# Feed forward of a decoder layer: rows transposed by DMA instead of TensorE, seven banks for gate and up, roundings on ScalarE

## The reference

```python
def _weight_quant(w):
    scale = 1.0 / clip(mean(abs(w)), 1e-05)
    return clip(round(w * scale), -1.0, 1.0) / scale
def _act_quant(x):
    scale = 127.0 / clip(max(abs(x), axis=-1, keepdims=True), 1e-05)
    return clip(round(x * scale), -128.0, 127.0) / scale
def _bitlinear(x, w):
    return einsum('bsi,oi->bso', _act_quant(x), _weight_quant(w))
gate = silu(_bitlinear(x, w_gate))
up = _bitlinear(x, w_up)
return _bitlinear(gate * up, w_down)
...
x = _layernorm(x + _L0_ffn_ref(x, L0_ffn_w_gate, L0_ffn_w_up, L0_ffn_w_down), axis=-1)
```

## Time and profile before

| | |
|---|---|
| runs | 1810.21, 1814.68 and 1814.8 us, median 1814.68 |
| the profiled execution | span 1810.6 us; the page gives no time of it beside the span |
| TensorE | busy 1764.0 us, 97% of the span |
| VectorE, ScalarE, GpSimd | 1422.3, 1182.3, 1120.8 us |
| critical chain by engine | PE 71%, issue 10%, POOL 7%, DVE 6%, DMA 4%, ACT 2% |
| TensorE's granted clock, mean | 0.995 of full speed |

### The profile page before, as it was taken

How to read it: one execution, slowest core, us unless ns; L and a number is a source line. 1 busy time by engine, 2 the same in 40 slices (tenths; PEclk the granted TensorE clock), 3 DMA queues, 4 the chain that set the end, 5 groups by cost and what they waited for, 6 DMA issues and landing times.

```text
span 1810.6 us, 43108 instructions
## 1 busy us (share of the span) xinstructions
PE 1764.0 (97%) x14196; PEld 1488.3 (82%) x14213; DVE 1422.3 (79%) x3304; ACT 1182.3 (65%) x2709; POOL 1120.8 (62%) x1250
## 2 busy tenths in 40 slices
PE   8999999999998899999999999999999999989997
PEld 7777777777777899999999999889999999975553
DVE  6777778787887677777777788777777777788998
ACT  6878887756755566666666667666666665665665
POOL 3434445664566586686686655678778778552554
PEclk9999999999998999999999999999999999999999
DMA  5222223111105422432432523314313341552221
GB/s 205 76 65 91 96 81 114 43 30 43 48 21 172 136 93 95 150 98 76 150 103 70 168 92 86 112 50 123 94 60 99 95 115 48 124 110 50 70 70 64
DMA packets 107012, 166.89 MB, mean 92 GB/s; under 512 B 29900, under 2 KB 65104, under 8 KB 106944
## 3 DMA queue, kind: packets, MB, share of 16 engines
q1 hardware_dynamic: 88408, 129.75, 23.3%
q0 software_dynamic: 14656, 28.92, 5.8%
q10 hardware_dynamic: 3880, 7.35, 1.3%
HBM read 109.25 MB, written 50.46 MB: 88 GB/s over the span
## 4 chain that ended last, share of the span: by engine, by line
PE 71%; issue 10%; POOL 7%; DVE 6%; DMA 4%; ACT 2%; POOLq 0%; ACTq 0%; DVEq 0%
PE att_ps_P L1737 5%; PE att_ps_SA L1761 5%; PE att_ps_T L554 5%; PE att_ps_P L1725 4%; PE att_ps_P L1789 4%; PE att_ps_P L554 3%; PE att_ps_O L1725 3%; PE att_ps_T L1725 3%; DMA ca_ct<-ct_kept 3%; PE att_ps_T L1737 3%; PE att_ps_SB L616 3%; POOL sa_p_lo L425 3%; PE att_ps_P L1775 3%; PE att_ps_SB L602 2%; PE att_ps_O L1737 2%
## 5 line engine op out<-in xcount | busy, mean ns | idle before, releaser
L1543 POOL TENSOR_TENSOR ca_pr<-ca_pr,ca_rec 112x750 f32<-112x750 f32 x256 | 366.5, 1452 | 186.4 <-DVE ca_rec L2023 183.3
L425 POOL TENSOR_TENSOR sa_p_lo<-sa_pr,sa_p_hi 112x448 fp32r<-112x448 f32 x128 | 147.1, 1164 | 210.0 <-ACT sa_p_hi L722 209.2
L1908 ACT ACTIVATE ca_big<-att_ps_P 126x384 fp32r<-126x384 f32 (+1 forms) x254 | 105.3, 449 | 66.2 <-PE att_ps_P L1775 64.8
L1902 ACT ACTIVATE ca_pr<-att_ps_SA,ca_nmax 112x750 f32<-112x750 f32 x128 | 113.7, 888 | 21.8 <-DVE ca_nmax L2019 11.0
L891 DVE RECIPROCAL sa_sums<-sa_sums 128x224 f32<-128x224 f32 x64 | 99.1, 1548 | 34.8 <-ACT sa_sums L731 34.6
L2028 DVE TENSOR_TENSOR ca_big<-att_ps_P,ca_big 126x384 fp32r<-126x384 f32 (+1 forms) x254 | 120.0, 500 | 6.2 <-ACT ca_big L1908 5.9
L2019 DVE TENSOR_REDUCE ca_nmax<-att_ps_SA 112x1 f32<-112x752 f32 x128 | 119.2, 931 | 1.3 <-PE att_ps_SA L1761 1.2
L2019 DVE TENSOR_REDUCE ca_nmax<-att_ps_SB 112x1 f32<-112x752 f32 x128 | 119.2, 931 | 0.0
L1737 PE MATMUL att_ps_P<-ca_w_hi,ca_ct 128*126 128x256 f32 x558 | 114.1, 283 | 1.4 <-DVE ca_q_lo L2002 1.4
L1902 ACT ACTIVATE ca_pr<-att_ps_SB,ca_nmax 112x750 f32<-112x750 f32 x128 | 113.3, 885 | 0.1
L1775 PEld LDWEIGHTS att_ps_P<-att_ident,ca_pr 64*126 64x126 f32 (+1 forms) x1524 | 85.8, 138 | 14.6 <-issue 10.8
(11 more groups left out here) (355 smaller groups left out, 6688.7 us busy)
## 6 DMA issues: line engine op xcount, KB each, us to landing
ct_kept<-ca_ct SPq DMA_DIRECT2D x8, 1134.0 KB, 8.9
ca_ct<-ct_kept POOLq DMA_DIRECT2D x8, 1134.0 KB, 8.0
ct_kept<-ca_ct SPq DMA_DIRECT2D x8, 1116.0 KB, 11.5
ca_ct<-ct_kept POOLq DMA_DIRECT2D x8, 1116.0 KB, 10.4
sa_xin<-in_x_dram SPq DMA_DIRECT2D x16, 448.0 KB, 3.6
xt_kept<-ca_xt SPq DMA_DIRECT2D x8, 896.0 KB, 5.2
ca_xt<-xt_kept POOLq DMA_DIRECT2D x8, 896.0 KB, 5.0
ternary<-ca_stage SPq DMA_DIRECT2D x36, 172.0 KB, 1.9
```

Source lines behind the costliest of these rows:

```text
L425: pool.tensor_tensor(p_lo[:, h % NB, :], pr[:, h % NB, :], f32(p_hi[:, h % NB, :]), ALU.subtract).then_inc(p_split, 1)
L1543: pool.tensor_tensor(w, w, rec[:, h % PB, c:c + 1].to_broadcast([R, S]), ALU.mult).then_inc(norm_done, 1)
L1902: act.activation(pr[:, h % PB, c, :].rearrange("r (a s) -> r a s", a=2), two_halves(psum[slot]), ACT.Exp, bias=nmax[:, h % PB, c:c + 1], a ...
```

## The change

In the feed forward only:

- Rows are transposed by transposing DMAs in SyncE's queue: turn_x (xq into one of two buffers xqt) for tiles 2 to 13, turn_hidden (each half of hq into hqt) for tiles 0 to 12. Tiles 0 and 1 still get x by TensorE, tile 13 its hidden rows (transpose_last, copy_last).
- Gate products have four banks, up products three: up 1 and up 3 share P1. A bank is used again by the same product of the next tile.
- The second half of hq is rounded by ScalarE (quantise_second), and from tile 3 on both steps of the rounding of x.
- The scales of all tiles have places of their own (amax, xscale, x_unit, hmax, hscale, h_unit by tile). res, y and y_out move to other addresses.
- The loops of VectorE, ScalarE, TensorE and SyncE are written out tile by tile. GpSimd's loop and its code stay. The new order on VectorE starts each pass with the residual and bn_stats of tile t - 2, and ends it with the aggregate and the guess.
- Some semaphores that only counted turns are merged or left out.

```diff
+    gate_ps = [psum["SB"][:, BANK:2 * BANK], psum["P0"], psum["SA"][:, BANK:2 * BANK], psum["O"]]
+    up_ps = [psum["T"], psum["P1"], psum["SB"][:, 0:BANK], psum["P1"]]
...
+    def before_x(t):
+
+        return xqt_in[(t - 1) % 2], 16 * ((t - 1) // 2)
...
+        def load_x(t):
+            if t:
+                sp.wait_ge(xr_done, t)
+            sp.dma_start(xin[:, :], x2[t * P:t * P + P, :]).then_inc(x_in, 16)
+
+        def load_residual(t):
+            sp.wait_ge(y_summed, t + 1)
+            sp.dma_start(res[:, :], x2[t * P:t * P + P, :]).then_inc(res_in, 16)
+
+        def turn_x(t):
+            sp.wait_ge(xq_done, t + 1)
+            sp.wait_ge(up_filled, FB * (t - 1))
+            sp.dma_start_transpose(xqt[:, t % 2], xq[:, :]).then_inc(xqt_in[t % 2], 16)
+
+        def turn_hidden(t, half):
+            sp.wait_ge(hq_done[half], t + 1)
+            if half == 0:
+                sp.wait_ge(y_filled, t + 1)
+            sp.dma_start_transpose(hqt[:, half * FC // 2:(half + 1) * FC // 2, :], hq[:, half_of(half)]).then_inc(hqt_in[half], 16)
...
         def load_fourth():
...
+            load_x(3)
+            turn_x(2)
+            turn_hidden(0, 0)
+            turn_hidden(0, 1)
 
         def rest():
...
+            for t in range(1, T):
+                if t > 1:
+                    turn_hidden(t - 1, 0)
+                load_residual(t - 1)
+                if t > 1:
+                    turn_hidden(t - 1, 1)
+                if 4 <= t + 3 < T:
+                    load_x(t + 3)
+                if t + 2 < T:
+                    turn_x(t + 2)
+            load_residual(T - 1)
...
         def gate_up(t, first, blocks):
...
+                    if not first and n == 7:
+                        pe.wait_ge(h_done, FB * t + 2)
+                    elif not first and n == 3:
+                        pe.wait_ge(h_done, FB * t)
+                    elif not first:
+                        pe.wait_ge(used, FB * (t - 1) + f + 1)
...
+        def rest():
+            pe.wait_ge(sg_done, FB)
+            for f in range(FB):
+                for ca_done in ca_free(f"v{f}"):
                     pe.wait_ge(*ca_done)
+                gate_up(1, False, [f])
+            pe.wait_ge(held[2], 16)
+            down(0)
+            for t in range(2, T):
+                gate_up(t, False, range(FB))
+                down(t - 1)
+            transpose_last()
             down(T - 1)
...
+        def quantise_second(t):
+            act.wait_ge(h_scaled, 2 * t + 2)
+            if t:
+                act.wait_ge(hqt_in[1], 16 * t)
+            act.activation(hq[:, half_of(1)], h[:, half_of(1)], ACT.Copy, bias=-ROUND).then_inc(hq_done[1], 1)
...
         def rest():
             copy_x(1)
...
+            for t in range(1, T):
+                scale_hidden(t - 1, 0)
+                scale_hidden(t - 1, 1)
+                quantise_second(t - 1)
+                silu(t, 0)
+                silu(t, 1)
+                if t + 2 < T:
+                    round_x(t + 2)
+                silu(t, 2)
+                if t + 2 < T:
+                    quantise_x(t + 2)
+                silu(t, 3)
...
+        def scale_of_hidden(t):
+            links.need(largest(t, 1))
+            links.link(dve.scalar_tensor_tensor(hmax[:, t, 0:1], hmax[:, t, 0:1], 1e-5, hmax[:, t, 1:2], ALU.max, ALU.max))
+            inverse = links.mark(dve.reciprocal(hscale[:, t:t + 1], hmax[:, t, 0:1]))
+            dve.tensor_scalar(h_unit[:, t:t + 1], wmean[:, 2:3], hmax[:, t, 0:1], 1.0 / 127.0, ALU.mult, ALU.mult)
+            links.need(inverse)
+            dve.tensor_scalar(hscale[:, t:t + 1], hscale[:, t:t + 1], 127.0, None, ALU.mult).then_inc(hscale_done, 1)
...
+        def sum_rows(t):
+            dve.wait_ge(y_free, t + 1)
+            add_residual(t, y)
+            dve.wait_ge(y_summed, t + 2)
+            dve.wait_ge(y_done, t + 1)
+            return links.mark(dve.bn_stats(stats[:, 0, :], y[:, :]))
+
+        def guess_root(sums):
+            dve.memset(rs[:, :], 0.0)
+            links.need(sums)
+            links.link(dve.bn_aggr(mv[:, 0, :], stats[:, 0, :]))
+            links.link(dve.tensor_scalar(mv[:, :, 1], mv[:, :, 1], LN_EPS, None, ALU.add))
+            links.link(dve.tensor_scalar(newton[:, :].bitcast(I32), mv[:, :, 1].bitcast(I32), 1, None, ALU.logical_shift_right))
             dve.tensor_scalar(rs[:, :].bitcast(I32), newton[:, :].bitcast(I32), -1.0, RSQRT_GUESS, ALU.mult, ALU.add).then_inc(guess_done, 1)
...
         def rest():
...
+            for t in range(2, T):
+                sums = sum_rows(t - 2)
+                if t + 2 < T:
+                    scale_of_x(t + 2)
+                hidden(t, 0)
+                hidden(t, 1)
+                hidden(t, 2)
+                largest(t, 0)
+                hidden(t, 3)
+                scale_of_hidden(t)
+                guess_root(sums)
+                quantise_hidden(t, 0)
+            quantise_hidden(T - 1, 1)
```

More of the change, by code:

```diff
@@ L2447, in copy_h, with silu @@
-        def copy_h(t, blocks):
-            for q in blocks:
-                act.wait_ge(ht_filled, FB * t + q + 1)
+            act.activation(xqt[:, t], xt_ps[:, :].rearrange("p (k n) -> p k n", k=KC), ACT.Copy).then_inc(xqt_done, 1)
+        def silu(t, f, first=False):
+            if f == 0:
+                act.wait_ge(x_scaled, t + 1)
+            act.wait_ge(gate_filled, FB * t + f + 1)
+            if FB * t + f >= 2:
+                act.wait_ge(h_done, FB * t + f - 1)
+            act.activation(sg[:, f % 2, :], gate_up_bank(f, 0, first)[:, :], ACT.Silu, scale=x_unit[:, t, 0:1]).then_inc(sg_done, 1)
@@ L2452, in copy_h @@
                 act.activation(hqt[:, 4 * q:4 * q + 4, :], ht_ps[q % 2][:, :].rearrange("p (k n) -> p k n", k=4),
                                ACT.Copy).then_inc(hqt_done, 1)
-        def scale_h(t, ahead=False):
-            act.wait_ge(hscale_done, t + 1)
-            for half in range(2):
-                if half and ahead:
-                    silu(t + 1, False, [0])
-                part_h = h[:, half * F // 2:(half + 1) * F // 2]
-                act.activation(part_h, part_h, ACT.Copy, scale=hscale[:, 0:1], bias=ROUND).then_inc(h_scaled, 1)
@@ L2534, in quantise_h, with quantise_hidden, add_residual @@
+        def quantise_hidden(t, half):
             dve.wait_ge(h_scaled, 2 * t + half + 1)
[L2535 to L2537 removed]
+            if t:
+                dve.wait_ge(hqt_in[half], 16 * t)
+            dve.tensor_scalar(hq[:, half_of(half)], h[:, half_of(half)], -ROUND, None, ALU.add).then_inc(hq_done[half], 1)
+        def add_residual(t, rows):
             dve.wait_ge(res_in, 16 * t + 16)
@@ L2592, in first @@
         def first(name):
             if name == "x":
-                dve.memset(h_unit[:, :], 0.0).then_inc(h_unit_clear, 1)
-                chain.step(lambda per, k: k)
                 scale_of_x(0)
             elif name == "xq":
+                round_x(0)
                 quantise_x(0)
-                take_unit(0)
             elif name == "next":
@@ L2602, in first @@
             elif name == "nextq":
-                dve.wait_ge(xt_filled, 1)
+                round_x(1)
                 quantise_x(1)
             elif name == "h":
-                dve.wait_ge(h_unit_clear, 1)
-                finish_h(0, statistics=False, next_hidden=False)
-            elif name == "v2":
-                chain.step(lambda per, k: FIRST + k)
-                hidden(1, 2)
-                largest(1, 0)
+                scale_of_hidden(0)
+                scale_of_x(2)
+                quantise_hidden(0, 0)
+                round_x(2)
+                quantise_x(2)
             elif name == "g":
-                finish_h(1, statistics=False)
+                scale_of_hidden(1)
+                quantise_hidden(1, 0)
             elif name[0] == "v":
-                dve.wait_ge(unit_done, 2)
-                hidden(1, int(name[1]))
+                f = int(name[1])
+                if f == 1:
+                    scale_of_x(3)
+                hidden(1, f)
+                if f == 2:
+                    largest(1, 0)
             else:
@@ L2621, in first @@
                     largest(0, 0)
[L2623 to L2649 removed]
+        def rest():
+            for t in range(2, T):
[11 more added lines that the diff above has]
+            quantise_hidden(T - 1, 1)
+            for i, rows in enumerate(last_rows):
+                t = T - 2 + i
+                add_residual(t, rows)
                 dve.wait_ge(y_summed, t + 2)
[L2651 removed]
+                layernorm(dve, links, [rows[:, :]], stats, last_mv, last_rs[:, :], last_newton[:, :], last_done)
         return first, rest
```

315 lines of the change are left out of this document (105 added, 210 removed).

## The result

The changed kernel took 1855.72 us in the median of four runs (1854.55 to 1856.46), the kernel before 1814.74 in the runs beside it; the ratio is 1.0234 with an interval of 1.0217 to 1.0251. The change costs 41 us. The profiled execution took 1856.46 us, its span is 1854.9.

A forecast was written before the change was run, and what follows sets the result against it. Bound now: TensorE; after: a ring of VectorE and GpSimd waits, 8.4 + 0.1 + 6.4 + 0.15 = 15.05 us a tile. Span 1810.6 + 43.4 = 1854.0, plus 4.1 to the median: 1858 us, range 1849 to 1876.

The forecast's parts named there:

- ring: Feed-forward loop: VectorE's guess, GpSimd's chain, next bn_stats, whole pass; 15.05 us a tile against 11.48; forecast given 0.82.
- The cover: Feed-forward loop: TensorE idle about 4.8 us a tile; half 1's transpose has 7.8 us against 4 taken.
- The start: Hand-over into feed forward: VectorE stands about 0.9 us for x; residual here at 1664.6, tile 0's bn_stats at 1665.4.
- The end: After the feed-forward loop: last scale done at 1838.65 against 1795.27; tail the same program, 15.3 us; span 1854.0.
- low bound of the range: Whole kernel: 1849, with -3 for the ring and 4 us either way for the loop's start and end.
- VectorE's busy time: Feed-forward tile: 10.56 less 0.68 for one hq rounding and some 1.2 for other work, 8.7 us.
- rival (a): Feed forward: the y_done wait costs nothing, TensorE stays the bound; 11 us less, 1804; chance 0.06.
- Transposes: SyncE's transposing DMAs: 0.14 us of queue a block; 4 us for half the hidden rows, bounds 1.5 and 9.
- Rival (b): Feed forward: transposing DMAs become the bound; worst 27 us a tile, about 2000; by the skill's price some 1990; chance 0.05.
- The clock: Feed-forward TensorE, idle 4.8 us a tile: some microseconds at half clock, +0.2 us a tile, in the upper end.
- rule weighed in the prediction: Feed-forward TensorE: idle gaps between matmul bursts send its clock to half rate, each tile begins slow; sum 1860.
- upper end: Feed-forward loop: includes +0.2 us a tile for TensorE's down products finishing later at half clock; sum 1860.

The follow-up runs named there:

- wait-moved version: Changed kernel with VectorE's wait for y_done moved from ahead of bn_stats to ahead of guess_root: 1810.4 us against 1813.9 for the kernel before, ratio 0.9973.

## Why the prediction was right

The forecast was 1858 us and a ring; 1855.7 came, by that ring.

- **Ring.** Forecast 15.05 us a tile, 15.10 in the mean. VectorE's part 8.4, measured 8.55: the third silu and h 3 came 0.1 later. GpSimd 6.4, measured 6.50, and 0.20 for two semaphores where 0.25 was put in. Two experiments on the length of GpSimd's chain, one on the wait and two on the kernel before show that it is this ring and the order that closes it.
- **The cover.** VectorE is ready at 1736.81 + 0.74 and waits to 1741.91; TensorE waits for h 1 ahead of the last up product. Forecast 4.8 us of idle TensorE, measured 3.4 in the mean of twelve waits (1.7 to 4.9), as its matmuls behind the lull were slower:

```profile
...
1729.94 1.89 PE L2420 MATMUL att_ps_P<-ff_held,ff_xqt 128*128 128x512 bf16 x4 [2.94 <-DVE ff_h L2574]
...
1731.62 4.10 PE L2443 MATMUL att_ps_SA<-ff_held,ff_hqt 128*128 128x512 bf16 x16
...
```

- **The start.** The residual's load: forecast 1661.07 + 0.9 = 1661.97, issued at 1662.51; bn_stats of tile 0 forecast at 1665.4, came at 1666.0. These 0.6 us, and ten passes of 15.2 against 15.05 (+1.7), are made up for by passes 12 and 13, which have no x to prepare and are 1.1 us shorter each; this I had not taken out. That the last scale was forecast to 0.02 us is luck: these errors cancel.
- **The end.** The last scale was to be done at 1838.65, it was at 1838.52 + 0.15 = 1838.67. From there to the end of the span it took 16.2 us, not 15.3: TensorE had stood 2.43 us ahead of the last transposes (1.06 in the kernel before), its clock fell to 0.50, and the 16 matmuls of down(13) took 4.70 us where they had taken 3.62.

```profile
...
1841.07 0.40 PE L2431 MATMUL att_ps_SB<-ff_ident_b,ff_hq 128*128 128x128 bf16 x4 [2.43 <-DVE ff_hq L2593]
...
1843.05 4.70 PE L2443 MATMUL att_ps_SA<-ff_held,ff_hqt 128*128 128x512 bf16 x16
```

```profile
...
1842.00:1844.00 2.00, 1.75 (x11) 1.14 (x12) 1.77 (x8) 1.68 (x4) 1.44 (x8) 0.50 0.29 80
...
```

The span came out at 1854.9 against 1854.0, 0.9 us longer than forecast. To get from the span to the median I added 4.1 us, and the median lay 0.8 above the profiled span: 3.3 too much. The two errors partly cancel and leave the 2.3 us by which 1858 was over. The low bound of the range was not what its terms give: 1858 - 3 - 4 is 1851, not 1849.
- **VectorE's busy time** was put at 8.7 us a tile and was 9.8. 0.45 us of the difference is its rounding, 1.13 us where 0.68 was put in; where the rest comes from I have not worked out. The forecast didn't hang on it, since the ring was added up from its own steps, but rival (a) did: with the ring opened VectorE's queue came to 10.83 us a tile, not 8.65.
- **Transposes.** I took 4 us to landing, between 1.5 and 9; it is 3.1 for eight blocks and 2.3 for four. The queue time of 0.14 us a block was right for eight (1.2 us) and half too low for four (1.2 as well). Rival (b) has no case here: from 4 to 8 blocks the landing grows by 0.8 us, 0.2 a block, near the weights' 0.175 and far from the 1.3 us that the Trainium skill (VectorE: DVE Perf Modes, The three transpose paths) gives for a block.
- **The clock.** The lull did lower it, as argued from the earlier trace rows: it is 0.89 over a pass, and the four matmuls of the last up product above take 1731.62 - 1729.94 = 1.68 us, 0.42 each, where one took 0.2155 before. This agrees with what the Trainium skill (TensorE: Matmul & The Clock Gate, Why this matters for your kernels) has on idle gaps between bursts; it is the rule weighed in the prediction, which names another section for it. But it cost the ring no more than 0.1 us a tile, half of the 0.2 in the upper end: passes with a slow last up product mostly take 15.25 us, the others 15.16, since nothing on the ring is TensorE's but that product.
- **Rival (a)** asked for the ring to be absent. With the ring opened the time is 1810, and with VectorE's idle time filled 1806, near the 1804 worked out for it.

What stays open: what the DMA transposes and the seven banks are worth apart from each other. The bank plan leaves no room for TensorE's transposes, and it wasn't tried.

## What to carry to other kernels

Before a step is moved in an in-order queue, list what its waits wait for and where in the same queue that chain is started: if the start now lies just ahead of the wait, the whole of the other engine's chain becomes part of each pass, however idle every engine looks. Then put each wait directly ahead of the instruction that overwrites what it protects, not ahead of the group; here that was worth 45 us of 1856. In a loop bound by such a ring, time taken off any engine outside it (here the 1.1 us of TensorE's transposes) shows nowhere until the ring is opened.

## What the runs showed of the hardware that was not expected

```profile
...
L2593 DVE TENSOR_SCALAR ff_hq<-ff_h 128x1024 bf16<-128x1024 f32 x9 | 10.1, 1127 | 4.9 <-ACT ff_h L2493 4.9
...
...
```

(The columns are busy us, mean ns of one, idle time before.) VectorE's rounding of 1024 columns to bf16 took 1.13 us here and 0.68 before. It now begins 0.45 us after GpSimd's subtraction of 512 columns, which kept its 1.03 us. In one pass of the wait-moved version GpSimd was late and began second:

```profile
...
1764.03 0.69 DVE L2593 TENSOR_SCALAR ff_hq<-ff_h 128x1024 bf16<-128x1024 f32 x1 [0.55 <-ACT ff_h L2493]
1765.71 0.75 DVE L2598 SCALAR_TENSOR_TENSOR ff_y<-att_ps_SA,ff_h_unit,ff_res 128x512 f32<-128x512 f32 x1 [0.98 <-POOLq L2377]
...
1775.50 1.13 DVE L2593 TENSOR_SCALAR ff_hq<-ff_h 128x1024 bf16<-128x1024 f32 x1 [0.55 <-ACT ff_h L2493]
...
```

```profile
...
1764.39 1.24 POOL L2376 TENSOR_TENSOR ff_y_out<-ff_y,ff_mv 128x512 f32<-128x512 f32 x1 [3.86 <-DMA out_dram<-ff_y_out]
...
```

There the rounding (1764.03) took 0.69 and the subtraction 1.24; at 1775.50, behind the subtraction again, it took 1.13. In another pass (rounding at 1708.87, subtraction at 1709.77) the two did not overlap and took 0.69 and 1.03. They don't run side by side at full rate, and in these passes it was the one that came second that was stretched, by 0.45 or 0.21 us. In the earlier trace rows it was GpSimd's small operations: the one at 1785.22 began 0.07 us behind a rounding and took 0.67 instead of 0.19. A transposing DMA held SyncE's queue 1.20 us for four blocks and 1.24 for eight: the price is by the instruction, not the block, at this size.
